# Shared-expert work moved between the pieces of the block tables, in a fused attention and mixture-of-experts kernel

## The reference

```
scores = softmax((x @ wt.T + g @ wg.T) / 2)               # 2048 tokens, 8 experts
topk_w, topk_idx = top_k(scores, 2);  topk_w /= topk_w.sum(-1)
y_all = (leaky(x @ w_gate[e]) * (x @ w_up[e])) @ w_down[e]  # for every expert e
y = sum over the two chosen experts of topk_w * y_all
p = leaky(x @ sw_gate) * (x @ sw_up) @ sw_down             # shared expert, 256 wide
y = y + p
s = y @ w_router                                           # then top 768 tokens of 1024:
out = x + where(chosen, gelu(y @ w_block), y)
```

## Time and profile before

| | us |
|---|---|
| median of 3 runs | 380.38 |
| the runs | 380.38, 381.49, 377.99 |
| profiled execution, its own time | 377.98 |
| profiled execution, span of the core | 376.1 |
| granted TensorE clock, share of full, whole span | 0.899 |

### The profile page before, as it was taken

The page is one execution under the profiler, slowest core; times in us unless marked ns, Lnnn a source line. Parts: engine busy times, 40 slices in busy tenths (PEclk is TensorE's granted clock), DMA queues, the critical chain, the costliest instruction groups (busy, mean ns, idle before and its releaser), DMA issues. The chain is left out here.

```text
span 376.1 us, 6114 instructions
## 1 busy us (share of the span) xinstructions
PE 309.6 (82%) x1659; PEld 214.1 (57%) x1659; DVE 220.5 (59%) x851; ACT 136.1 (36%) x428; POOL 151.3 (40%) x244
## 2 busy tenths in 40 slices
PE   7799999979988879768388179879999999864970
PEld 6366676546764644344174145458877786553850
DVE  4564445333632746366245758848655553699996
ACT  1365767552010741626021000015555554034420
POOL 1349989770030004161500377774565556000000
PEclk9999999999999975568769779989999999969895
DMA  5969920000059400000010032645555431660014
GB/s 153 292 139 323 298 93 3 2 1 2 0 179 264 105 0 0 2 0 0 7 46 1 34 107 99 182 127 147 161 160 164 127 105 44 208 240 3 2 59 164
DMA packets 36074, 38.01 MB, mean 101 GB/s; under 512 B 5182, under 2 KB 31679, under 8 KB 36034
## 3 DMA queue, kind: packets, MB, share of 16 engines
q1 hardware_dynamic: 31650, 29.04, 28.4%
q0 software_dynamic: 3408, 8.43, 6.1%
q10 hardware_dynamic: 976, 0.08, 0.2%
HBM read 21.88 MB, written 16.57 MB: 102 GB/s over the span
## 5 line engine op out<-in xcount | busy, mean ns | idle before, releaser
L2406 POOL DMA_INDIRECT YS<-XY,IB x39 | 38.4, 985 | 28.3 <-DVE IB L2811 17.1
L2505 PE MATMUL psU<-WGU,XT 128*128 x156 | 42.3, 395 | 0.1
L2619 ACT COPY XT<-psG 128x256 f32<-128x256 f32 x39 | 14.7, 377 | 51.0 <-PE psG L2495 50.7
L1193 POOL TENSOR_SCALAR UU<-UU,rs 128x257 f32<-128x257 f32 x32 | 29.9, 935 | 0.0
L2505 PEld LDWEIGHTS psU<-WGU,XT 128*128 128x128 f32 x156 | 27.3, 195 | 3.5 <-issue 0.7
L1360 ACT ACTIVATE UU<-UU,nm 128x129 f32<-128x129 f32 x64 | 28.4, 452 | 0.7 <-DVE nm L1469 0.7
L1469 DVE CUSTOM_DVE_ANT_0 UU<-psS,BI 128x129 f32<-128x129 f32 x64 | 19.1, 356 | 14.3 <-PE psS L1248 14.3
L2437 PE MATMUL psY<-SD,HH 128*128 128x256 f32 x64 | 16.9, 410 | 12.7 <-DVE HH L2780 12.7
L2380 POOL DMA_INDIRECT XS<-AI,SI x16 | 16.0, 1002 | 26.6 <-DVE SI L2727 22.0
L2819 DVE TENSOR_SCALAR LK<-psU 128x128 f32<-128x128 f32 x39 | 11.4, 291 | 24.3 <-PE psU L2505 24.3
L1192 POOL TENSOR_SCALAR UU<-UU,rs 128x129 f32<-128x129 f32 x32 | 19.7, 615 | 13.5 <-DVE rs L1479 13.4
(11 more groups left out here) (342 smaller groups left out, 722.6 us busy)
## 6 DMA issues: line engine op xcount, KB each, us to landing
XS<-PZ SPq DMA_DIRECT2D x1, 5011.5 KB, 20.7
XY<-XS SPq DMA_DIRECT2D x39, 128.5 KB, 2.5
YR<-YS SPq DMA_DIRECT2D x2, 1028.0 KB, 6.8
BI<-in_bias SPq DMA_DIRECT2D x4, 512.0 KB, 8.8
X<-in_x SPq DMA_DIRECT2D x2, 768.0 KB, 10.1
out_dram<-X SPq DMA_DIRECT2D x3, 512.0 KB, 3.0
WGU<-YS SPq DMA_DIRECT2D x1, 1028.0 KB, 10.3
XY<-YS SPq DMA_DIRECT2D x1, 1028.0 KB, 12.4
```

Of the source, the lines that this page charges most:

```text
L1193: pool.tensor_scalar(U[:, he, W1:WU], U[:, he, W1:WU], rs[:, d, 2 * he + 1:2 * he + 2], None, ALU.mult).then_inc(n_done, 1)
L2406: pool.indirect_dma_start(YS[:, :], bass.IndirectOffsetOnAxis(ap=IB[:, b, n:n + 1], axis=0), YB[i][:, n, :], None, bounds_check=2 * NTOK - ...
L2505: mm = pe.matmul(psU[b % 2][:, n * D:(n + 1) * D], XT[b % 2][:, k, n * P:(n + 1) * P], WGU[:, k, bass.ds(which[b], 1), :].rearrange("p a m ...
```

## The change

Only the order of instructions changes; none is added or taken away.

1. DVE: `table(w)` is cut in three functions (`table_counts`, `table_experts`, `table_rows`), and what stood between it and the shared jobs in two more (`whole_blocks`, `choice_weights`). `leaky_product(0)` now stands straight behind `SI`; the pieces of the tables lie between the shared jobs; `table_rows(2)` and `choice_weights` have moved into the block loop, at b = 2 and b = 3.
2. PE: the wait for the first table stands at n = 2 and no more at n = 1. `read_experts` takes at most two registers per shared job, and in the block loop one per block, six blocks ahead (before: 17 registers during the shared jobs, then one per block from step 13 on). The wait for the third `shared_result` and for the eight columns moves from before the first `turned` to step 3, before the first `narrow`.
3. POOL: the last four token scatters (second choice of tiles 12 to 15) alternate with the result scatters of blocks 0 to 3.

The diff, cut to its core (in the new functions the instructions are those of before):

```diff
@@ POOL
-                    first_choice(0)
-                    first_choice(1)
-                    second_choice(0, 0)
-                    second_choice(1, 1)
-                    first_choice(2)
-                    first_choice(3)
-                    second_choice(2, 2)
-                    second_choice(3, 3)
-
-                    for b in range(NBK):
...
+                    def result_rows(b):
                         pool.wait_ge(s_ib, b + 1)
                         pool.wait_ge(yb_done, b + 1)
...
+                    for t in range(2 * TT):
+                        first_choice(t)
+                    for c in range(2):
+                        second_homes(c, c)
+                        for t in range(TT * c, TT * c + TT):
+                            second_choice(t)
+                    for t in range(2 * TT, 3 * TT):
+                        first_choice(t)
+                    for t in range(3 * TT, NT):
+                        first_choice(t)
+                    second_homes(2, 2)
+                    for t in range(2 * TT, 3 * TT):
+                        second_choice(t)
+                    second_homes(3, 3)
+                    for i in range(TT):
+                        result_rows(i)
+                        second_choice(3 * TT + i)
+                    for b in range(TT, NBK):
+                        result_rows(b)
@@ PE
                     for n in range(NF):
                         if n >= 1 and n + 1 < NF:
                             gate_up(n + 1)
-                        if n == 1:
+                        if n == 2:
                             pe.wait_ge(s_route, TABLE[0])
-                        read_experts(min(5 * n, READY[0]) if n < 4 else READY[1])
+                        read_experts(max(0, 2 * n - 4))
                         down(n)
...
-                    pe.wait_ge(y_done, NC_ - 1)
-                    pe.wait_ge(s_side, SIDE_COLUMN)
                     for i in range(NBK + 3):
-                        read_experts(max(READY[1], i + 5))
+                        read_experts(i + 6)
...
+                        if i == 3:
+                            pe.wait_ge(y_done, NC_ - 1)
+                            pe.wait_ge(s_side, SIDE_COLUMN)
                         if i >= 3:
                             narrow(i - 3)
@@ DVE
-                    for n in range(NF + 1):
-                        if n < NF:
-                            leaky_product(n)
-                            column_product(n)
-                        if n >= NS_ and n % NS_ == 0:
-                            shared_result(n // NS_ - 1)
-                        if n in (2, 4):
-                            table(n // 2)
-                    for n in range(NF, E):
-                        column_product(n)
+                    leaky_product(0)
+                    whole_blocks()
+                    table_counts(0)
+                    leaky_product(1)
+                    table_experts(0)
+                    table_rows(0)
+                    dve.wait_ge(s_wb, 32)
+                    column_product(0)
+                    column_product(1)
+                    leaky_product(2)
+                    column_product(2)
+                    shared_result(0)
+                    table_counts(1)
+                    leaky_product(3)
+                    column_product(3)
+                    table_experts(1)
+                    table_rows(1)
+                    leaky_product(4)
+                    column_product(4)
+                    shared_result(1)
+                    table_counts(2)
+                    leaky_product(5)
+                    column_product(5)
+                    table_experts(2)
+                    column_product(6)
+                    column_product(7)
+                    shared_result(2)
                     dve.wait_ge(y_done, NC_ - 1)
                     dve.wait_ge(s_side, SIDE_COLUMN)
                     for b in range(NBK + 1):
+                        if b == 2:
+                            table_rows(2)
+                        if b == 3:
+                            choice_weights()
                         if 1 <= b <= NT - TT:
                             score_product(b - 1)
```

More of the change, by code:

```diff
@@ L2376, in _, with first_choice, second_homes @@
                     pool.wait_ge(s_route, SLOT_IDS)
-                    def first_choice(c):
-                        for t in range(TT * c, TT * c + TT):
-                            pool.indirect_dma_start(XS[:, :], bass.IndirectOffsetOnAxis(ap=SI[:, 0, t:t + 1], axis=0),
-                                                    AI[:, t, :], None).then_inc(s_first[c], 16)
-                    def second_choice(c, turn):
+                    def first_choice(t):
+                        pool.indirect_dma_start(XS[:, :], bass.IndirectOffsetOnAxis(ap=SI[:, 0, t:t + 1], axis=0),
+                                                AI[:, t, :], None).then_inc(s_first[t // TT], 16)
+                    def second_homes(c, turn):
                         pool.wait_ge(s_first[c], 16 * TT)
@@ L2396, in _, with second_choice @@
[L2396 to L2402 removed]
+                    def second_choice(t):
+                        pool.indirect_dma_start(XS[:, :], bass.IndirectOffsetOnAxis(ap=SI[:, 1, t:t + 1], axis=0),
+                                                AI[:, t, :], None).then_inc(s_second[(0, 0, 1, 2)[t // TT]], 16)
@@ L2727, in _, with whole_blocks, size, table_counts @@
                     dve.tensor_copy(SI[:, :, :], SF[:, :, :]).then_inc(s_route, 1)
-                    for w in range(2):
-                        chain(dve.tensor_tensor(CMP[0:1, :, :], early_n[:, w, :].unsqueeze(2).broadcast_to([1, E, NT]),
-                                                fill_f[0:1, :].unsqueeze(1).broadcast_to([1, E, NT]), ALU.is_gt), True)
-                        chain(dve.tensor_reduce(whole[:, w, :], CMP[0:1, :, :], AX_X, ALU.add), True)
-                    chain(dve.tensor_copy(whole[:, 2, :], nbk[0:1, :]))
-                    chain(dve.memset(given[:, :], 0.0), True)
-                    def table(w):
-                        lo = READY[w - 1] if w else 0
-                        m = READY[w] - lo
-                        new = slice(lo, lo + m)
+                    def whole_blocks():
+                        for w in range(2):
+                            chain(dve.tensor_tensor(CMP[0:1, :, :], early_n[:, w, :].unsqueeze(2).broadcast_to([1, E, NT]),
+                                                    fill_f[0:1, :].unsqueeze(1).broadcast_to([1, E, NT]), ALU.is_gt), True)
+                            chain(dve.tensor_reduce(whole[:, w, :], CMP[0:1, :, :], AX_X, ALU.add), True)
+                        chain(dve.tensor_copy(whole[:, 2, :], nbk[0:1, :]))
+                        chain(dve.memset(given[:, :], 0.0), True)
+                    def size(w):
+                        return READY[w] - (READY[w - 1] if w else 0)
+                    def table_counts(w):
                         chain(dve.tensor_tensor(waiting[:, :], whole[:, w, :], given[:, :], ALU.subtract), True)
@@ L2761, in table, with choice_weights @@
                             chain(dve.tensor_tensor(given[:, :], given[:, :], ahead[:, :], ALU.add), True)
-                    table(0)
-                    chain(dve.scalar_tensor_tensor(out=R1[:, :], in0=top_s[:, 0, :], scalar=1e-20, in1=top_s[:, 1, :],
-                                                   op0=ALU.add, op1=ALU.add), True)
-                    chain(dve.reciprocal(R1[:, :], R1[:, :]), True)
-                    for k in range(2):
-                        chain(dve.tensor_tensor(W2[:, k, :], top_s[:, k, :], R1[:, :], ALU.mult))
-                    dve.wait_ge(s_wb, 32)
-                    chain(dve.tensor_copy(need[:, :], need_i[:, :]))
-                    chain(dve.memset(cnt[:, :, :], 0.0), True)
+                    def choice_weights():
+                        chain(dve.scalar_tensor_tensor(out=R1[:, :], in0=top_s[:, 0, :], scalar=1e-20, in1=top_s[:, 1, :],
+                                                       op0=ALU.add, op1=ALU.add), True)
+                        chain(dve.reciprocal(R1[:, :], R1[:, :]), True)
+                        for k in range(2):
+                            chain(dve.tensor_tensor(W2[:, k, :], top_s[:, k, :], R1[:, :], ALU.mult))
+                        chain(dve.tensor_copy(need[:, :], need_i[:, :]))
+                        chain(dve.memset(cnt[:, :, :], 0.0), True)
                     def leaky_product(n):
```

21 lines of the change are left out of this document (10 added, 11 removed).

## The result

The changed kernel takes **372.44 us** (median of 20 runs, 369.03 to 377.03); the kernel before takes 379.94 (20 runs, 374.07 to 384.0). The ratio is 0.9835, 95% interval 0.9802 to 0.9868, so the gain is 1.3 to 2.0%. The two medians lie 7.5 us apart and the ratio says 6.3, because the medians are over all runs and the ratio leaves out those more than 1.5% above the fastest of their kernel. The forecast was 372.7, with 369.3 to 377.0. The profiled execution of the changed kernel took 372.11 us, its span 370.3.

What follows compares the result with a forecast made beforehand. PE was taken to bound the blocks, so an earlier start means an earlier end. Terms -9.0 + 1.1 + 0.7 + 0.4 = -6.8 us, against the mean of 379.5, gave 372.7 us, range 369.3 to 377.

Steps and rivals of the forecast that it cites:

- First `down`, 5.35 us earlier: Start of the shared jobs: `leaky_product(0)` directly behind `SI` comes 5.35 us earlier, so `down(0)` starts at about 213.15.
- `turned(0)`, -9.0: From first `down` to first block: `turned(0)` starts at 239.6 in place of 248.57, a gain of 9.0 us.
- I keep the slow restart of before in it: Shared jobs: PE's clock after the idle stretch, now 4.9 us, was assumed to restart as slowly as before.
- up to 0.7 us more: Shared jobs: the extra gain if PE's clock stayed at 2.4 GHz through the shorter idle stretch.
- Loads, 11 x 0.10 = +1.1: Block loop: 11 more register loads than before, at 0.10 us each, cost 1.1 us.
- The rival of 0.6 us each: Block loop: each of 11 extra register loads costs 0.6 us, 6.6 us in all, giving 378.2 us; chance 0.10.
- the slower case with 0.92: Block loop: each of 11 extra loads costs SP's 0.92 us, 10.1 in all, giving 381.7 us; chance 0.05.
- DVE in the first blocks, +0.7: First blocks: two moved DVE jobs hold PE up by 1.3 us, a faster clock returns 0.6; bounds -0.4 and +2.0.
- POOL, +0.4 at block 9: Result buffers: ACT waits 0 to 1.6 us for block 9's buffer, partly absorbed by its idle time, costing 0.4 us.
- POOL's ring decides: Result buffers: landing takes 3.7 us throughout and ACT's wait reaches PE in full, giving 375.6 us; chance 0.15.
- What would show it: Signs: `down(0)` at 213.2, `turned(0)` at 239 to 240, no column wait, blocks 1.73 us apart from the start.
- if early steps take over 2 us: Early blocks: a stated sign that the prediction is wrong, steps there longer than 2 us.

Runs made afterwards that it cites:

- r1: The kernel before with only VectorE's new order, run again on a chip with the usual time: 377.51 us, ratio 0.9926 to the kernel before.
- e2_pe_only: The kernel before with only TensorE's new order (later reads, later waits), on the chip with the stall: 402.45 us, ratio 0.9982 to the kernel before.
- e8_warm: The changed kernel plus five unused matmuls in PE's idle stretch before `down(0)`: 374.16 us, ratio 0.9891 to the kernel before.
- e5: The changed kernel with the register reads back where they stood before: 374.12 us, ratio 0.9895 to the kernel before.
- e1: The kernel before with only VectorE's new order, on the chip with the stall: 399.11 us, ratio 0.989 to the kernel before.
- e6: The changed kernel with `table_rows(2)` back in the shared jobs and `choice_weights` at block 14: 373.35 us, ratio 0.9876 to the kernel before.
- e7: The changed kernel with twelve result buffers in two groups of six, in place of six: 370.85 us, ratio 0.9803 to the kernel before.
- r3: The changed kernel with GpSimd's old order (no alternation), on a chip with the usual time: 373.51 us, ratio 0.986 to the kernel before.
- r4: The changed kernel with PE's waits for copy and columns back before the first block, usual-time chip: 371.84 us, ratio 0.9775 to the kernel before.
- e9: The changed kernel with five unused matmuls, twelve result buffers, and `table_rows(2)` and `choice_weights` out of the first blocks: 370.77 us, ratio 0.9773 to the kernel before.

## Why the prediction was right

The time and the main mechanism held: the first shared job had stood behind small jobs that nobody on PE's path needed, and moving it brings the first block forward, by 4.3 us alone (`r1`) and by 8.0 with PE's edits beside it. That the sum came so close is in part luck, since its errors cancel. By its own steps, against the profile and the experiments:

1. *First `down`, 5.35 us earlier.* Measured 7.85 - 2.37 = 5.48, and the same in every kernel with VectorE's new order.
2. *`turned(0)`, -9.0.* Measured -8.03. This is the term with the largest error. DVE's order ran as computed; `down(5)` waits 0.58 us for `HH` (0.5 predicted), and the 2.21 us for copy and column are gone. What was off is "I keep the slow restart of before in it". From `down(0)` to `down(5)` it takes 25.68 us, and 24.55 were computed; 1.05 of this is the clock, 0.50 and then 0.66 in the first two stretches of 3 us, where the profile of before had 0.51 and 1.00. But that profile is one with an early return, and `e2_pe_only` with the same idle time has 0.69. In the profiles with the new order the second stretch lies between 0.64 and 0.91. So the forecast took one execution's luck for the price of a restart. Nor is "up to 0.7 us more" right for a clock that stays up: `e8_warm` has block 0 at 27.74, which is 10.17 us earlier than before and 1.2 more than the 9.0.
3. *Loads, 11 x 0.10 = +1.1.* Confirmed by the difference of blocks 5 to 13 (+0.83 for 8 loads, and back by the same with `e5`). The rival of 0.6 us each, and the slower case with 0.92, are refuted for loads that stand alone between blocks: the longest idle time of PE that is put down to issue there is 0.42 us, once, at block 3. Where five loads can begin only behind a late table, they cost more, up to 0.69 us each (3.46 to 3.48 us from the table to `down(1)` in `e1`, `r1` and `e5`). The Trainium skill, "DMA: Bandwidth & Descriptors", Latency and other measured facts, gives a floor of about 600 ns for a tensor_load. These three traces do not contradict it; what the 0.10 us shows is that such a time is hidden when PE has work ahead of the load.
4. *DVE in the first blocks, +0.7.* Blocks 0 to 5 are 0.60 longer, where 1.1 stood in the forecast (0.4 for four loads, 0.7 here). The full clock that was set against the jobs is there (1.00 where it was 0.62). How the 0.60 is made up is not shown: without the loads it is 0.25 less (`e5`), with the jobs moved 0.28 less (`e6`), and profiles differ by 0.28 there without an edit that reaches these blocks.
5. *POOL, +0.4 at block 9.* The place and the size were both off. The last token scatter was issued at 258.66 and held nobody up. At block 9 ACT waited 0.54 us, within the 0 to 1.6 that was computed, and PE did not notice. But result 8's scatter took 5.54 us to land, where 2.06 to 3.7 stood in the prediction, and held block 18 up by 0.94. Why it took so long, no run tells. It is still not the rival "POOL's ring decides": `e7` takes the wait away and gets 0.2 us. The alternation, for which the prediction saw a use at block 6, shows none: `r3` moves the wait and changes nothing in the sum.
6. *Not foreseen.* Blocks 18 to 38 are 0.73 us shorter, of which one load less explains 0.1. In the other kernels of the study blocks 18 to 35 take 28.7 to 29.2 us, as after the change (28.87), and 29.6 in the one profile of before, so it may be that profile that is long. No run tells it apart.
7. *What would show it.* Most signs came: `down(0)` at 213.57, block 0 at 241.08 (29.88 behind `SI`, and 28.9 was forecast), no wait for a column, no wait of PE for a block's data, the clock at 1.00 in the blocks. One sign of being wrong came too: "if early steps take over 2 us". The steps from block 3 to 4 and from 4 to 5 took 2.53 and 2.02 us, and the blocks are not 1.73 us apart from the start. It did not decide the case, since the shorter steps around them (1.95 and less) leave the 0.60 of point 4.

The terms measured from `SI` add up to 101.72 - 95.58 = 6.1 us at the last block, where 6.8 was forecast, and the runs' ratio gives 379.94 x (1 - 0.9835) = 6.3 us (5.0 to 7.5). The difference of 0.7 us is made up of +1.0 up to block 0, -0.5 in blocks 0 to 5 (0.60 for 1.1), nothing in 5 to 13, +0.8 in 13 to 18 (1.19 for the ring's 0.4), and -0.6 in 18 to 38 (-0.73 for -0.1). Two of these, the first and the last, may belong to the one profile of before and not to the change. The median came within 0.3 us of the forecast also because the base, 379.5, lay 0.4 below the median of the longer series.

What the parts are worth: VectorE's order gives 0.9926 alone, and all three together 0.9835; these two intervals do not overlap. That TensorE's edits pay only beside VectorE's is argued from the two waits in `r1`, not shown by a time: alone they were run only on the chip with the stall (0.9982), and taken back one at a time (`e5`, `r4`) they leave a kernel whose time is not above the change's beyond the intervals.

## What to carry to other kernels

Look behind the instruction that everyone waits for: small jobs that stand between it and the first consumer's work cost their whole length if a bound engine is idle (5.5 us here), and can cost a small part of it where the engine that runs them has slack. A wait that costs nothing today (for a table with the register reads behind it, for a copy) comes onto the path as soon as the wait ahead of it is gone, so move both in one change. And price a buffer ring by the *longest* landing in the trace, not the usual one, then test whether taking the wait away moves the last block, before counting it. Compare the clock of two profiles stretch by stretch before a difference under a microsecond is put down to an edit.

## What the runs showed of the hardware

- The time from issue to landing of the same kind of indirect scatter, one of many in flight, went from 2.08 us (the last result scatter after the change) to 5.54 (result 8). Its cause is open.
- A register load in PE's list costs 0.10 us between two blocks (0.82 us for eight, `e5`), and up to 0.69 us where five follow a table that comes late (3.47 us in `r1`).
- After 4.88 us of idleness PE's clock is 0.50 for 3 us, and the moment of its return differs between profiles with the same instructions there: 0.64 to 0.91 in the second three microseconds, which moves all that follows by up to 0.8 us. After 10.35 us of idleness it is 1.00 in the profile of before and 0.69 in `e2_pe_only`, 0.9 us apart. Five matmuls in the gap, which leave 0.48 us of idleness, keep it at 1.00 (`e8`, `e9`).
- One chip took 6% longer for the same program, 404.39 against 379.9 us, with a stall of DVE of 20 to 26 us in the shared jobs that the profile puts down to "remote". Its cause is open, and a comparison made there says little of the stretch that it covers.
